# Feed-forward weights read transposed from the host arrays, without transposes on TensorE

## The reference, cut to what matters

```python
xf = x.reshape(-1, x.shape[-1])                       # 1024 x 512
up = jnp.einsum('td,fd->tf', xf, W_up)                # W_up   1376 x 512
gate = jax.nn.silu(jnp.einsum('td,fd->tf', xf, W_gate))   # W_gate 1376 x 512
h = gate * up
y = jnp.einsum('tf,df->td', h, W_down)                # W_down 512 x 1376
```

## Time and profile before

| | |
|---|---|
| time, median of 3 runs | 1029.48 us (1028.76 to 1030.11) |
| profiled execution, span from the first to the last instruction | 1029.7 us |
| mean granted TensorE clock | 0.992 of full speed |
| PE busy | 1003.1 us, 97% of the span |
| DVE, ACT, POOL busy | 581.3, 428.1, 381.6 us |
| feed-forward stage, first to last instruction | about 828.6 to 1029.7 us, 201 us |

### The profile page before, as it was taken

One profiled execution on the slowest core, in us unless ns is written; L12 is line 12 of the kernel. 1 busy time (PEld: TensorE's weight loads), 2 busy tenths in 40 slices (PEclk: granted clock), 3 DMA queues, 4 the chain that ended last, 5 costly groups with the idle time before them and its releaser, 6 DMA issues. The chain is left out here.

```text
span 1029.7 us, 16071 instructions
## 1 busy us (share of the span) xinstructions
PE 1003.1 (97%) x5260; PEld 822.9 (80%) x5260; DVE 581.3 (56%) x973; ACT 428.1 (42%) x1239; POOL 381.6 (37%) x375
## 2 busy tenths in 40 slices
PE   5999999989999999999999999999999999999998
PEld 3787777876888888888888888888887778888787
DVE  3765555636776666767666666766765852222101
ACT  2777666751533433533533434434334433332100
POOL 7422222253642642643634534626424222222100
PEclk8999999989999999999999999999999999999999
DMA  6000000211110210210210201201100022221001
GB/s 199 12 11 11 11 10 10 62 52 52 50 54 1 73 32 0 71 31 0 74 27 20 72 10 31 61 10 49 43 1 32 1 62 61 61 69 47 11 31 41
DMA packets 45699, 39.98 MB, mean 39 GB/s; under 512 B 3617, under 2 KB 34465, under 8 KB 45665
## 3 DMA queue, kind: packets, MB, share of 16 engines
q1 hardware_dynamic: 45280, 38.48, 12.7%
q0 software_dynamic: 384, 1.05, 0.3%
HBM read 37.43 MB, written 2.10 MB: 38 GB/s over the span
## 5 line engine op out<-in xcount | busy, mean ns | idle before, releaser
L624 PE MATMUL bank<-cross_wo_hl,cross_outT_hl 128*128 128x512 f32 x768 | 191.7, 398 | 1.0 <-POOL cross_wo_hl L618 0.6
L624 PE MATMUL bank<-hsT_hl,cross_wqkv_hl 128*128 128x512 f32 x768 | 188.2, 394 | 0.0
L624 PEld LDWEIGHTS bank<-cross_wo_hl,cross_outT_hl 128*128 128x128 f32 x768 | 143.1, 188 | 35.5 <-POOL cross_wo_hl L618 1.6
L624 PEld LDWEIGHTS bank<-hsT_hl,cross_wqkv_hl 128*128 128x128 f32 x768 | 141.9, 188 | 29.3
L938 ACT ACTIVATE cross_scores<-cross_scores,cross_negmax 128x128 f32<-128x128 f32 x256 | 99.8, 391 | 127.1 <-DVE cross_negmax L876 127.1
L798 POOL TENSOR_TENSOR cross_qT<-rotated,rotated_other_half 128x512 f32<-128x512 f32 x64 | 82.8, 1293 | 162.0 <-DVE rotated_other_half L840 162.0
L624 PE MATMUL bank<-hsT_hl,ff_gate_upT_hl 128*128 128x512 f32 (+1 forms) x528 | 126.3, 395 | 0.5 <-DVE ff_gate_upT_hl L1140 0.5
L624 PEld LDWEIGHTS bank<-hsT_hl,ff_gate_upT_hl 128*128 128x128 f32 (+1 forms) x528 | 96.3, 186 | 21.9 <-DVE ff_gate_upT_hl L1140 0.8
L948 ACT CAST cross_outT_hl<-bank 128x512 fp32r<-128x512 f32 x64 | 37.1, 579 | 143.4 <-PE bank L624 142.5
L838 DVE TENSOR_TENSOR rotated<-bank,cosT 128x512 f32<-128x512 f32 x80 | 55.2, 690 | 71.4 <-PE bank L624 71.2
L624 PE MATMUL bank<-ctxT_hl,cross_wqkv_hl 128*128 128x512 f32 x384 | 94.3, 394 | 1.1 <-PEq L74 1.1
(11 more groups left out here) (121 smaller groups left out, 1565.7 us busy)
## 6 DMA issues: line engine op xcount, KB each, us to landing
staged_rows<-in_wq SPq DMA_DIRECT2D x32, 256.0 KB, 2.8
staged_rows<-in_wo SPq DMA_DIRECT2D x32, 256.0 KB, 2.7
staged_rows<-in_wg SPq DMA_DIRECT2D x10, 256.0 KB, 2.6
staged_rows<-in_wu SPq DMA_DIRECT2D x10, 256.0 KB, 2.8
staged_rows<-in_wd SPq DMA_DIRECT2D x10, 256.0 KB, 3.0
ctx_tok<-in_ctx SPq DMA_DIRECT2D x8, 256.0 KB, 2.6
staged_rows<-in_wk SPq DMA_DIRECT2D x8, 256.0 KB, 3.1
staged_rows<-in_wv SPq DMA_DIRECT2D x8, 256.0 KB, 3.1
```

Source lines behind the costliest of these rows:

```text
L624: i = nc.tensor.matmul(out, stationary[:, a], moving[:, b], start=(first and k == 0), stop=(last and k == 2))
```

## The change

The host hands `W_gate`, `W_up` and `W_down` over transposed. SP therefore loads the tiles in the layout that the products want: gate and up as 4 x 128 runs of 128 numbers, and down as 128 whole rows of 512 numbers. All 132 transposes on PE go, with the banks `TW` and `TD` and the semaphores `w_transposed` and `wd_transposed`. ACT and DVE read the staged tiles in SBUF where they read PSUM banks. ACT waits for the load itself, and the next load into a slot waits until DVE's subtraction has read it (`w_low`, `wd_low`), where it waited until PE's transposes had.

```diff
@@ load_ff_rows
     for k, name in enumerate(("wg", "wu")):
         if not (isinstance(i, int) and i == 0):
-            sp.wait_ge(sem["w_transposed"], 2 * i + k - 1)
-            if k == 1:
-                sp.wait_ge(sem["wd_transposed"], i)
-        sp.dma_start(m["gate_up_rows"][0:n, k, :], io[name][bass.ds(at, n), :]).then_inc(sem[f"{name}_loaded"], 16)
-    sp.dma_start(m["down_rows"][:, :, 0:n], io["wd"].rearrange("(t p) f -> p t f", p=P)[:, :, bass.ds(at, n)]).then_inc(sem["wd_loaded"], 16)
+            sp.wait_ge(sem["w_low"], 2 * i + k - 1)
+        sp.dma_start(m["gate_up_rows"][:, k, :, 0:n], io[name].rearrange("(t p) f -> p t f", p=P)[:, :, bass.ds(at, n)]).then_inc(sem[f"{name}_loaded"], 16)
+    if not (isinstance(i, int) and i == 0):
+        sp.wait_ge(sem["wd_low"], i)
+    sp.dma_start(m["down_rows"][0:n, :], io["wd"][bass.ds(at, n), :]).then_inc(sem["wd_loaded"], 16)
@@ feed_forward, vector
-                nc.vector.tensor_tensor(wT[:, k, 1, :, 0:n], TW[k][:].rearrange("p (t f) -> p t f", t=KT)[:, :, 0:n],
+                nc.vector.tensor_tensor(wT[:, k, 1, :, 0:n], raw[:, k, :, 0:n],
                                         wT[:, k, 0, :, 0:n].bitcast(F32), ALU.subtract).then_inc(sem["w_low"], 1)
-                nc.vector.tensor_tensor(wdT[0:n, 1, bass.ds(i, 1), :], TD[0:n, :].unsqueeze(1), wdT[0:n, 0, bass.ds(i, 1), :].bitcast(F32),
+                nc.vector.tensor_tensor(wdT[0:n, 1, bass.ds(i, 1), :], rawd[0:n, :].unsqueeze(1), wdT[0:n, 0, bass.ds(i, 1), :].bitcast(F32),
                                         ALU.subtract).then_inc(sem["wd_low"], 1)
@@ feed_forward, scalar
-                act.wait_ge(sem["w_transposed"], 2 * i + k + 1)
+                act.wait_ge(sem["wu_loaded" if k else "wg_loaded"], 16 * i + 16)
                 if not first:
                     act.wait_ge(sem["ff_product"], products_by(i - 1, k, 1))
-                nc.scalar.copy(wT[:, k, 0, :, 0:n], TW[k][:].rearrange("p (t f) -> p t f", t=KT)[:, :, 0:n]).then_inc(sem["w_high"], 1)
+                nc.scalar.copy(wT[:, k, 0, :, 0:n], raw[:, k, :, 0:n]).then_inc(sem["w_high"], 1)
-                act.wait_ge(sem["wd_transposed"], i + 1)
-                nc.scalar.copy(wdT[0:n, 0, bass.ds(i, 1), :], TD[0:n, :].unsqueeze(1)).then_inc(sem["wd_high"], 1)
+                act.wait_ge(sem["wd_loaded"], 16 * i + 16)
+                nc.scalar.copy(wdT[0:n, 0, bass.ds(i, 1), :], rawd[0:n, :].unsqueeze(1)).then_inc(sem["wd_high"], 1)
@@ feed_forward, tensor
-            def w_transposes(i, k, first=False):
...
-                for t in range(KT):
-                    e = nc.tensor.transpose(TW[k][:, t * P:t * P + n], raw[0:n, k, t * P:(t + 1) * P], ident[0:n, 0:n])
-                e.then_inc(sem["w_transposed"], 1)
             def body(i, first=False):
-                n = width_of(i)
-                w_transposes(i, 1, first)
-                pe.wait_ge(sem["wd_loaded"], 16 * i + 16)
...
-                for t in range(KT):
-                    e = nc.tensor.transpose(TD[0:n, t * P:(t + 1) * P], rawd[:, t, 0:n], ident[:])
-                e.then_inc(sem["wd_transposed"], 1)
...
                 product(i, 0)
-                if not (isinstance(i, int) and i == FT - 1):
-                    w_transposes(i + 1, 0)
                 product(i, 1)
-            w_transposes(0, 0, first=True)
             body(0, first=True)
@@ kernel
-    given["pos"] = _np.ascontiguousarray(given["pos"].T)
+    for name in ("pos", "wg", "wu", "wd"):
+        given[name] = _np.ascontiguousarray(given[name].T)
```

More of the change, by code:

```diff
@@ L1082, in feed_forward @@
 def feed_forward(nc, m, sem, ps, io):
-    GATE, UP, TW, TD, YB = ps[0:2], ps[2:4], ps[4:6], ps[6], [ps[7], ps[6]]
-    x, hsT, ident, raw, rawd = m["x"], m["hsT_hl"], m["ident"], m["gate_up_rows"], m["down_rows"]
+    GATE, UP, YB = ps[0:2], ps[2:4], [ps[7], ps[6]]
+    x, hsT, raw, rawd = m["x"], m["hsT_hl"], m["gate_up_rows"], m["down_rows"]
     LATE = {7: GATE[1], 8: UP[1], 9: YB[0]}
@@ L1212, in _ @@
         def _(pe):
-            def w_transposes(i, k, first=False):
-                n = width_of(i)
-                pe.wait_ge(sem["wg_loaded" if k == 0 else "wu_loaded"], 16 * i + 16)
-                if not first:
-                    pe.wait_ge(sem["w_low"], 2 * i + k - 1)
-                for t in range(KT):
-                    e = nc.tensor.transpose(TW[k][:, t * P:t * P + n], raw[0:n, k, t * P:(t + 1) * P], ident[0:n, 0:n])
-                e.then_inc(sem["w_transposed"], 1)
             def product(i, k, first=False, halves=(0, 1)):
@@ L1233, in body @@
             def body(i, first=False):
-                n = width_of(i)
-                w_transposes(i, 1, first)
-                pe.wait_ge(sem["wd_loaded"], 16 * i + 16)
-                if not first:
-                    pe.wait_ge(sem["wd_low"], i)
-                for t in range(KT):
-                    e = nc.tensor.transpose(TD[0:n, t * P:(t + 1) * P], rawd[:, t, 0:n], ident[:])
-                e.then_inc(sem["wd_transposed"], 1)
                 if first:
@@ L1285 @@
 norm_stats norm_mv norm_var_eps norm_rstd norm_rows norm_transposed norm_high norm_low wg_loaded wu_loaded wd_loaded
-w_transposed w_high w_low wd_transposed wd_high wd_low ff_product silu h_product h_high h_low y3 x3""".split() + [f"piece_loaded{slot}" for slot in range(SLOTS)]
+w_high w_low wd_high wd_low ff_product silu h_product h_high h_low y3 x3""".split() + [f"piece_loaded{slot}" for slot in range(SLOTS)]
 def program(nc, io):
@@ L1298, in program @@
             "stage": stage,
-            "gate_up_rows": stage[:, 0:2, :],
-            "down_rows": stage[:, 2, :].rearrange("p (t f) -> p t f", t=KT),
+            "gate_up_rows": stage[:, 0:2, :].rearrange("p k (t f) -> p k t f", t=KT),
+            "down_rows": stage[:, 2, :],
             "norm_rows": stage[:, 3:5, :],
```

## The result

The changed kernel takes 1016.0 us in the median of 4 runs (1015.4 to 1016.8), against 1029.8 us of the kernel before beside it. The ratio of the runs is 0.9862, with a 95% interval from 0.985 to 0.9874, which is 14.2 us less (13.0 to 15.4); the two medians themselves differ by 13.8 us. The forecast was 1017.0 us with a range of 1015.0 to 1018.9, and a gain of 12.5 us. The profiled execution took 1015.9 us; its span is 1014.1, so the time of an execution is 1.8 us above its span here. For the kernel before the span of 1029.7 us was taken for the execution's own time. By the same 1.8 us that execution took about 1031.5 us (an estimate); since the forecast comes down to the median of the runs less 12.5 us, this does not change it.

What follows compares the result with a forecast made beforehand. PE's list of work was taken to bound the feed-forward stage. From the 1029.7 us span, -12.9 for transposes and +0.4 at the entry gave 1017.2, less 0.2 for the median: 1017.0 us, range 1015.0 to 1018.9.

Steps and rivals of the forecast that it cites:

- What bounds the stage: Feed-forward stage from 835.47 us on: it takes as long as PE's list of work, with 0.0 us idle before matmuls.
- What goes, 12.9 us: 30 groups of four PE transposes in the chain from 840.96 to 955.49 us vanish, saving 12.9 us.
- Do the products close up without a gap?: PE products where transposes stood: they follow each other without a gap, charged nothing; 0.05 us at 20 places only in range.
- Do the halves come in time: ACT's casts and DVE's subtractions per block: up's low half ready at T + 2.7, 2.8 us to spare, T ending product(i-1, up).
- The loads: Weight loads into slots freed after DVE's subtraction: land in 3.0 us with 12.4 us of room, so cost nothing.
- The entry, +0.4 us: Entry into the feed-forward stage: starts 0.38 us earlier, but DVE and POOL holds in SBUF make it 0.4 us later.
- one more hold of 0.69: Entry: POOL's last pair (L648, L650) held by L659 and new subtractions, putting the last L659 at about 834.6 us.
- the lower bound of -0.38: Entry term's low end: DVE's first subtraction and all following steps come 0.38 us earlier.
- the one without a hold: Rival: DVE and POOL do not hold each other up, the entry gains its 0.38 us; 1016.2 us, chance 0.32.
- Partial closing: Rival: gaps of 0.1 to 0.3 us between products at 20 places where transposes stood; 1019 to 1023 us, chance 0.07.
- The halves as the bound: Rival: weight halves take over 5.49 us after a product, so PE waits in each block; 1025 us, chance 0.04.
- late loads: Rival: ACT's cast of up(i+1) waits for its load; 1043 us at 15.0 us landing; chance 0.04, with other slower mechanisms.

Runs made afterwards that it cites:

- The six operations: The changed kernel with six unread statistics operations on DVE ahead of the subtraction of up in blocks 1 to 10: 1027.1 us, ratio 0.9962.

## Why the prediction was right, point by point

- **What bounds the stage:** right. Put the transposes back without readers and the stretch is 191.1 us again, and the time that of the kernel before (0.9999).
- **What goes, 12.9 us:** right in mechanism, too small by 1.0 us; it measured 13.9. The step that failed is "Do the products close up without a gap?". I asked only whether a closed place could cost something, and put 0.05 us for each of 20 places on the loss side. It is a gain: a place costs PE 0.04 to 0.05 us beyond its transposes. The sign stood in my own paragraph, 0.229 us a matmul between transposes and 0.228 without, though not the whole size: from these rows the difference is 0.001 us for each of 444 matmuls, 0.4 us. Blocks are 10.88 us apart (854.85 to 865.73) and not 10.98. With 5.44 us for a product instead of 5.49, the sum over 18.5 products gives the missing 0.9.
- **Do the halves come in time:** right. The hold is about as long as forecast (the subtraction ends at T + 3.5, forecast 3.67, with T = 852.83), and PE does not wait. Only its form was forecast wrong: the held subtraction does not begin after L1127 has ended but right after the cast, and is recorded as 1.50 us long. The six operations show where it would.
- **The loads:** right. They land in 2.9 us of the 12.4 that they have. No run made the loads late, so where PE would begin to wait for them is not shown.
- **The entry, +0.4 us:** wrong in sign, it measured -0.4. The hold is real, and the step that failed is "one more hold of 0.69". It took a held operation to cost the chain its whole length. The held ones were POOL's two small operations, by 0.36 and 0.34 us, and behind the second of them the last L659 had to wait for the third subtraction anyway. The room for it stood in the earlier trace rows: L650 ended 0.45 us before the last L659, so that even a hold of 0.69 us would have cost about 0.3 us (an estimate: 0.69 - 0.45 + 0.06). So the lower bound of -0.38 was the right value. The Trainium skill ("SBUF — State Buffer", section "Who interferes with whom") is borne out in that two SBUF inputs on DVE and a reading POOL operation hold each other up. It says that the later one waits for the whole instruction. That is a little too strong for these traces, as far as their spans on POOL can be trusted: L1140 ended 0.56 us after L1127, where it needs 0.67 or more by itself, and L1147 began while L650 was running and still took its usual 0.69 us.
- **Sum:** -12.9 + 0.4 was -13.9 - 0.4, an error of 1.8 us, in two terms of one sign. The time itself was off by 1.0 us only. That is in part luck. From the median that the forecast started at, 1029.5 - 14.3 would be 1015.2 us; but the kernel before had a median of 1029.8 us in this comparison, and the other 0.5 us are scatter between runs. The range had room for both times at its low end, though it was put there for other reasons.
- **The rivals:** the one without a hold had the better time (1016.2) for the wrong reason. Partial closing had the wrong sign. The halves as the bound and late loads did not come.

## What to carry to other kernels

On an engine that is never idle, price an instruction by the pieces of the chain, and its neighbours with and without it: here a group of transposes took 0.44 us and each place 0.05 more, 1.0 us of 13.9. When both engines that share a resource get new work there, ask not only how long one is held but what it stands behind afterwards; 0.8 us of hold on DVE and 0.7 on POOL cost nothing here, the latter by less than 0.1 us. And where work that waited for nobody is taken off an engine ahead of a wait, look at the idle gap that it leaves.

## What the runs showed of the hardware

- A DVE subtraction with two inputs in SBUF took 0.69 us alone and 1.50 beside POOL's 1.29 us operation; beside such a subtraction POOL's small operations took 0.55 and 0.89 us instead of 0.19 and 0.55. With one input in PSUM the subtraction beside the 1.30 us operation took 0.69 us, and the second small operation 0.55.
- Behind an idle gap of 3.85 us on PE the granted clock was 0.51 and all 5 executions had a lower mean. Behind 2.67 us it was 1.00 in most profiles, 0.66 and 0.50 in two. Behind 1.05 us, 12 transposes and another 0.12 us it was 1.00.
- A product of 24 matmuls took 5.44 us between products and 5.49 between transposes. Which matmul is the slower one the records don't show.
